# When the indirect writes of a routed block leave the GpSimd queue

## The chip, the cores and the metric

The kernel runs on one core of a Trainium2 chip. The metric is the device time of one execution in microseconds (us). A core has five engines with a queue each: TensorE (PE in the profile, its weight loads PEld), VectorE (DVE), ScalarE (ACT), GpSimd (POOL) and SyncE (SP, here only for DMAs). Each runs its queue in order, and they meet at semaphores.

## The reference, cut to what matters

16 sequences of 512 rows with 128 features are normalised and go through two branches, whose sum is added to the input: attention with 16 heads of 64, and a layer of 8 experts of which each row uses two.

```python
xn = layernorm(x)                                     # (16, 512, 128)
h = rmsnorm(xn) * norm_scale
q, k, v = h @ wq, h @ wk, h @ wv                      # 16 heads of 64
attn = softmax(q * 64**-0.5 @ k.T) @ v @ w_out + b_out
logits = silu(xn @ rw1 + rb1) @ rw2 + rb2             # the router, 8 experts
k_prob = softmax(top2(logits))
ffn = sum over the two chosen e of k_prob * (silu(xn @ w1[e] + b1[e]) @ w2[e] + b2[e])
out = x + attn + ffn
```

## The kernel before, in words

**Groups.** The program is written as 262 groups, `group(G)`. Of these, 256 carry attention: a batch has 16 groups (`GB`), a pair of heads has two (even and odd), and each group does two of the four tiles of 128 query rows. For each tile t: `scores` (PE, L394) fills two banks of PSUM; `maxima` (DVE, L403) reduces both to negated maxima NM; `probs` (ACT, L409) makes two tiles of exponentials; and in the group after, `turn_probs` (PE, L424) turns these with 16 transposes of 64x64, which ACT or DVE copies into PT (L436, L439). `weighted` (L453) multiplies PT by V. `project` (kq, L238 to L240) makes the next pair's queries or keys. Below, S0 and S1 are the scores of a group's two tiles, T0 and T1 the transposes of the group before, turned in between, and the first and second maximum those over S0 and S1.

**Order on TensorE.** `PE_ORDER` is written by hand: even groups run S0 T0 S1 T1 kq spread attend ... route, odd ones S0 T0 S1 ahead spread T1 route kq attend ... weighted. DVE and ACT have such lists too (`DVE_ORDER`, `ACT_ORDER`); POOL and SP take their work in the order in which it is added. PSUM banks are given out by a planner (`take`, with the costs in `HOLD`) as the work is added.

**The routed half.** In the groups 0 to 127, block r of 512 rows is routed over 8 groups, h = G mod 8, in `route(G)`. Groups h = 0 and 2: two chunks each of the router's first layer (`router`: PE L238 to L240 with XT, ACT tanh and bias, then on POOL `TH` L561 and `HS` L563). h = 3: `stats` of block r + 1 (DVE, then a POW on POOL, L284). h = 5 and 6: logits. h = 7: the first choice, and `turn_x(r + 1)` (PE, L338), which needs the first product of `routed_rows`. One block later, at h = 0 and 1, the second choice and `place` (DVE) make for each row its place in the list of its expert, and a flag (`gate` 24, L660) says that the places are there.

**The writes.** `scatter(r - 1, part)` then writes the rows of block r - 1 into the experts' lists in DRAM (`slots`): eight indirect DMAs from POOL (L664), one for each of the two choices and each of four tiles of 128 rows, 132 floats a row. They go out three in group h = 2, three in h = 3 and two in h = 4, all behind the flag alone. `routed_rows(r + 1)` (POOL, L307 to L313: three passes over 512 elements and two iotas) follows in h = 4. Its first instruction waits until all eight writes have landed, since it overwrites the rows that they read. In odd groups `route` is added ahead of `attend`, so every second block `attention_rows` (POOL, L298 and L300) stands behind `routed_rows`.

**Other work on POOL.** In the groups 24 to 57 (blocks 3 to 6 and the start of 7) `splitting` prepares the experts' weights; in even groups its subtraction (`SPL` L264) stands ahead of the writes. After the last routed block, in group 130, the eight writes of block 15 go out at once. From group 138 on the experts run beside attention, with accumulating indirect writes from POOL (L813, L534).

```python
elif 2 <= h <= 4:
    scatter(r - 1, slice(3 * h - 6, 3 * h - 3))   # 3, 3, 2 writes
...
if h == 4:
    routed_rows(r + 1)
```

Of the kernel before, what the change touches and what calls it, by code (L numbers as in the profile page):

```python
# [22 lines left out]
QT = S // P  # L23
# [42 lines left out]
class Queues:  # L66
# [7 lines left out]
    def add(self, engine, make, needs=(), name=None, step=1, sem=None, place="side"):  # L74
        key = None
        if name is not None:
            key = sem or (engine + "_" + name[0])
            self.count.setdefault(key, 0)
        self.open[engine].append((place, make, [n for n in needs if n is not None], name, key, step))
# [23 lines left out]
def block_kernel(nc, x, wq, wk, wv, wout, ns, bout, rw1, rb1, rw2, rb2, w1, w2, bias, ident, tri, consts, out):  # L103
# [11 lines left out]
    with ExitStack() as ctx:  # L115
# [111 lines left out]
        def load_q(r):  # L227
            if r < NB:
                add("sp", lambda e: e.dma_start(XQ[:, r % 2], xv[r]), needs=[("xc", r - 2), ("bn", r - 2)] if r >= 2 else [],
                    name=("xq", r), step=16, sem=f"xq_{r % 2}")  # L230
# [42 lines left out]
        def stats(r):  # L273
            for t in range(QT):
                add("dve", lambda e, t=t: e.bn_stats(bn[:, t, :], XQ[:, r % 2, t, :]),
                    needs=[("xq", r), ("mv", r - 1) if r else None], name=("bn", r))
            for t in range(QT):
                add("dve", lambda e, t=t: e.bn_aggr(mv[:, r, t, :], bn[:, t, :]), needs=[("bn", r)], name=("mv", r))
            old = ("pow", r - 1) if r else None
            add("dve", lambda e: e.tensor_scalar(sqi[:, 0:QT], mv[:, r, :, 1], 1.0, 1e-5, ALU.mult, ALU.add),  # L280
                needs=[("mv", r), old], name=("var", r, 0))
            add("dve", lambda e: e.tensor_scalar(sqi[:, QT:2 * QT], mv[:, r, :, 1], 1.0 + 1e-6, 1e-11, ALU.mult, ALU.add),
                needs=[("mv", r), old], name=("var", r, 1))
            add("pool", lambda e: e.tensor_tensor(sqo[:, r], sqi[:], HALF[:], ALU.pow), needs=[("var", r, 1), ("half",)],  # L284
                name=("pow", r))
# [16 lines left out]
        def routed_rows(r):  # L302
            mean = mv[:, r, :, 0:1].to_broadcast(full)
            rx = sqo[:, r, 0:QT].unsqueeze(2).to_broadcast(full)
            a, c = (XR[:, r % 2, k, :, 0:D] for k in range(2))
            old = [("sc", r - 2), ("xT", r - 2)] if r >= 2 else []
            add("pool", lambda e: e.tensor_tensor(c, XQ[:, r % 2], mean, ALU.subtract), needs=[("mv", r), ("xq", r), *old],  # L307
                name=("xc", r))
            add("pool", lambda e: e.tensor_tensor(a, c, rx, ALU.mult), needs=[("xc", r), ("pow", r), *old], name=("xr", r, 0))
            add("pool", lambda e: e.tensor_tensor(c, c, rx, ALU.mult), needs=[("xr", r, 0)], name=("xr", r, 1))  # L310
            for k in range(2):
                tok = XR[:, r % 2, k, :, D:D + 1].bitcast(I32)
                add("pool", lambda e, tok=tok: e.iota(tok, [[P, QT], [0, 1]], base=r * S, channel_multiplier=1),  # L313
                    needs=[*old, ("spare",)], name=("tok", r))
# [234 lines left out]
        def router(r, c):  # L549
            bk = xbank("r1")  # L550
            w = [R1[:, k, c * P:(c + 1) * P] for k in range(2)]
            m = [XT[:, k, :] for k in range(2)]
            add("pe", lambda e: three(e, bank[bk], w, m), needs=[("xTs", r, 1), ("wlo", "r1", 0), freed.get(bk)],
                name=("r1", r, c))
            add("act", lambda e: e.activation(TH[:, c % 2, :], bank[bk], ACT.Tanh, bias=RB1H[:, c:c + 1], scale=0.5),
                needs=[("r1", r, c), ("rb1h",), ("hs", r, c - 2) if c >= 2 else (("hs", r - 1, c + 2) if r else None)],
                name=("th", r, c))
            add("act", lambda e: e.activation(HS[:, c, :], bank[bk], ACT.Identity, bias=RB1[:, c:c + 1]),  # L558
                needs=[("r1", r, c), ("load", "rb1"), ("lg", r - 1) if r else None], name=("hz", r, c))
            freed[bk] = ("hz", r, c)  # L560
            add("pool", lambda e: e.tensor_tensor(TH[:, c % 2, :], TH[:, c % 2, :], HS[:, c, :], ALU.mult),  # L561
                needs=[("th", r, c), ("hz", r, c)], name=("tz", r, c))
            add("pool", lambda e: e.tensor_tensor(HS[:, c, :], HS[:, c, :], TH[:, c % 2, :], ALU.add),  # L563
                needs=[("tz", r, c)], name=("hs", r, c))

        def logits(r):
            bk = xbank("lg")

            def make(e):
                for c in range(NC):  # L570
                    m = e.matmul(bank[bk][32 * c:32 * c + 32, :], R2[:, c, :], HS[:, c, :], start=True, stop=True,
                                 tile_position=(0, 32 * c))
                return m

            add("pe", make, needs=[("hs", r, NC - 1), ("load", "r2"), freed.get(bk)], name=("lg", r))
            add("dve", lambda e: e.tensor_scalar(LG4[:], bank[bk], 0.5, RB2[:], ALU.mult, ALU.add),
                needs=[("lg", r), ("load", "rb2"), ("lgT", r - 1) if r else None], name=("lgs", r))
            freed[bk] = ("lgs", r)
# [3 lines left out]
        def turn_logits(r):  # L582
            bk = xbank("lgT")

            def make(e):
                for t in range(QT):
                    m = e.transpose(bank[bk][:, t * P:(t + 1) * P], LG4[:, t * P:(t + 1) * P], idn[:])
                return m

            add("pe", make, needs=[("lgs", r), ("load", "id"), freed.get(bk)], name=("lgT", r))  # L590
            parts = bank[bk].rearrange("p (t c e) -> p t e c", t=QT, c=NC)[:, :, 0:E]
            add("dve", lambda e: e.tensor_reduce(LG[:], parts, AX.X, ALU.add),
                needs=[("lgT", r), ("gate", r - 1, 6) if r else None], name=("gate", r, 0))
            freed[bk] = ("gate", r, 0)
# [64 lines left out]
                    needs=[("tanh", r), ("spare",), ("sc", r - 2) if r >= 2 else None], name=("wt", r, k))  # L659
            add("dve", lambda e: e.tensor_copy(junk[:, 2:3], junk[:, 0:1]), needs=[("to", r, 1), ("wt", r, 1)], name=("gate", r, 24))  # L660

        def scatter(r, part):
            for k, t in list(itertools.product(range(2), range(QT)))[part]:
                add("pool", lambda e, k=k, t=t: e.indirect_dma_start(  # L664
                    slots, bass.IndirectOffsetOnAxis(ap=IDX[:, r % 2, k, t:t + 1], axis=0), XR[:, r % 2, k, t, :], None),
                    needs=[("gate", r, 24), ("tok", r), ("xr", r, 1)], name=("sc", r), step=16, sem=f"sc_{r % 2}")

# [181 lines left out]
        for k in range(WARM):  # L851
            add("pe", lambda e: e.matmul(bank[7][:, 0:256], PR[:, 7, 0:P], PR[:, 7, 0:256], start=True, stop=True),
                needs=[("ones",)], name=("warm",))
# [8 lines left out]
        for key in (True, False):  # L862
# [12 lines left out]
            needs=[("pad0",)], name=("pad",))  # L875
# [56 lines left out]
        def route(G):  # L932
            r, h = divmod(G, 8)
            if 0 < r <= NB:
                if h == 0:
                    choose(r - 1, 1)
                    choose(r - 1, 2)
                if h == 1:
                    place(r - 1)
                if r == NB:  # L940
                    if h == 2:
                        scatter(r - 1, slice(0, 8))
                elif 2 <= h <= 4:
                    scatter(r - 1, slice(3 * h - 6, 3 * h - 3))
            if r >= NB:
                return
            if h in (0, 2):
                router(r, h)
                router(r, h + 1)
            if h == 5:  # L950
                logits(r)
                load_q(r + 2)
            if h == 6:
                turn_logits(r)
            if h == 7:
                choose(r, 0)
            if r + 1 < NB:
                if h == 3:
                    stats(r + 1)
                if h == 4:  # L960
                    routed_rows(r + 1)
                if h == 7:
                    turn_x(r + 1)
# [178 lines left out]
```

How the kernel before makes its waits and increments, by code:

```python
    def emit(self, engine, eng, sems):  # L91
        seen = {}
        for make, needs, key, step in self.items[engine]:
            for sem, value in (self.value[n] for n in needs):
                if seen.get(sem, 0) < value:
                    eng.wait_ge(sems[sem], value)
                    seen[sem] = value
            ins = make(eng)
            if key is not None:
                ins.then_inc(sems[key], step)
# [974 lines left out]
        @block.sync  # L1075
        def _(eng):
            q.emit("sp", eng, sems)
            for k, v in q.count.items():
                if k.startswith(("st_", "sadd", "spare_out", "base", "rrow", "tab", "b_tab", "sc_", "pads")):
                    eng.wait_ge(sems[k], v)
```

## Time and profile before

| | |
|---|---|
| three runs | 2043.05 to 2044.08 us, median 2043.65 us |
| profiled execution | 2040.24 us |
| its span, first to last instruction | 2038.4 us |
| mean granted TensorE clock | 0.990 |
| PE busy | 1947.9 us (96%) |
| DVE busy | 1539.4 us (76%) |
| ACT busy | 1574.2 us (77%) |
| POOL busy | 918.2 us (45%) |
| indirect writes to `slots` (L664) | 128, 125.8 us in all, 983 ns each |

Busy time is the union of an engine's instructions. The ends of matmuls are modelled in the profile, so when a result really was there is read from the engine that waits for it. The span of an indirect write on POOL is the time in which POOL prepares the transfer, not that of the transfer itself.

### The profile page before, as it was taken

How to read it: one execution, taken by the hardware profiler on the slowest of the kernel's cores; microseconds unless marked ns; L12 is line 12 of the kernel's file. 1: busy time of each engine (PE TensorE's matmuls, PEld its weight loads, DVE VectorE, ACT ScalarE, POOL GpSimd, SP SyncE). 2: the span in 40 equal slices, each digit the busy share in tenths (PEclk: the TensorE clock that was granted, in tenths of full speed). 3: DMA queues.
4: the chain of work that ended last, by engine and by line, in shares of the span. 5: the costliest groups of instructions: out<-in, count | busy, mean ns of one | idle time of the engine just before them, and what ended most of it. 6: DMA issues, size and time to landing. Idle time of an engine off the chain costs nothing.

```text
span 2038.4 us, 45230 instructions
## 1 busy us (share of the span) xinstructions
PE 1947.9 (96%) x16646; PEld 1254.4 (62%) x16646; DVE 1539.4 (76%) x2654; ACT 1574.2 (77%) x3716; POOL 918.2 (45%) x790
## 2 busy tenths in 40 slices
PE   7999999999999999998889999999999999999997
PEld 5655555555656555564556666666666666666664
DVE  6878888887878777776767777777777777777774
ACT  5777777777777777775678888888888888888884
POOL 4344455453344444441014645546446455464454
PEclk9999999999999999999999999999999999999999
DMA  2023222221111111001313334344333343343332
GB/s 84 30 61 103 91 98 89 85 72 34 40 37 43 38 43 38 33 32 36 91 57 81 84 86 84 80 95 85 85 79 85 86 83 88 84 85 80 79 75 47
DMA packets 132697, 141.96 MB, mean 70 GB/s; under 512 B 25438, under 2 KB 99038, under 8 KB 132446
## 3 DMA queue, kind: packets, MB, share of 16 engines
q1 hardware_dynamic: 101886, 118.34, 18.4%
q0 software_dynamic: 30592, 20.73, 8.6%
q8 instruction: 134, 2.20, 0.5%
q14 instruction: 85, 0.70, 0.1%
HBM read 102.65 MB, written 38.46 MB: 69 GB/s over the span
## 4 chain that ended last, share of the span: by engine, by line
PE 75%; ACT 12%; DVE 6%; issue 4%; DMA 2%; another core or an unknown queue 1%; SPq 0%; POOL 0%; POOLq 0%; DVEq 0%; ACTq 0%
PE pair L453 21%; PE pair L394 15%; PE pair L424 10%; PE pair L238 6%; PE pair L240 5%; PE pair L239 4%; ACT PR L409 4%; PE pair L499 2%; PE pair L501 2%; DVE NM L403 2%; PE pair L787 1%; PE pair L788 1%; PE pair L786 1%; ACT PT L436 1%; ACT HS L558 1%
## 5 line engine op out<-in xcount | busy, mean ns | idle before, releaser
L409 ACT ACTIVATE PR<-pair,NM 128x512 f32<-128x512 f32 x1024 | 718.2, 722 | 21.3 <-DVE NM L403 18.8
L403 DVE TENSOR_REDUCE NM<-pair 128x2 f32<-128x1024 f32 x512 | 611.8, 1211 | 68.0 <-PE pair L394 47.9
L436 ACT COPY PT<-pair 128x512 f32<-128x512 f32 x640 | 358.2, 608 | 368.4 <-PE pair L424 364.4
L394 PE MATMUL pair<-KS,QS 64*128 64x512 f32 x3072 | 491.7, 424 | 20.5 <-DVE KS L379 12.3
L453 PE MATMUL pair<-PT,V 128*64 128x512 f32 x2048 | 471.0, 602 | 0.2
L424 PEld LDWEIGHTS pair<-idn,PR 64*128 64x128 f32 x8192 | 338.0, 139 | 100.8 <-ACT HS L558 27.0
L394 PEld LDWEIGHTS pair<-KS,QS 64*128 64x128 f32 x3072 | 257.8, 188 | 181.1 <-issue 126.2
L424 PE MATMUL pair<-idn,PR 64*128 64x64 f32 x8192 | 343.2, 223 | 21.0 <-ACT HS L558 15.9
L813 POOL DMA_INDIRECT out<-YS,IDW x156 | 246.9, 1583 | 187.2 <-DVE YS L805 128.6
L778 POOL TENSOR_TENSOR HH<-ZZ,HH 128x512 fp32r<-128x512 f32 x156 | 199.2, 1347 | 291.1 <-ACT HH L775 291.1
L453 PEld LDWEIGHTS pair<-PT,V 128*64 128x64 f32 x2048 | 136.4, 137 | 258.7 <-issue 252.5
L439 DVE COPY PT<-pair 128x512 f32<-128x512 f32 x384 | 250.8, 681 | 14.7 <-remote 9.6
L409 ACT ACTIVATION_READ_ACCUMULATOR PR<-pair,NM 128x1 f32 x1024 | 242.1, 236 | 0.0
L561 POOL TENSOR_TENSOR TH<-TH,HS 128x512 f32<-128x512 f32 x64 | 81.8, 1278 | 295.9 <-ACT HS L558 295.6
L459 DVE TENSOR_TENSOR OT<-pair,RB 128x512 f32<-128x512 f32 x128 | 88.4, 690 | 144.8 <-PE pair L453 136.2
L772 DVE SCALAR_TENSOR_TENSOR ZZ<-ZT,ZZ 128x512 f32<-128x512 f32 x156 | 110.5, 709 | 79.2 <-ACT ZZ L763 79.1
L664 POOL DMA_INDIRECT slots<-XR,IDX x128 | 125.8, 983 | 89.9 <-DVE junk L660 58.8
L379 DVE TENSOR_TENSOR QS<-pair,QS 128x512 fp32r<-128x512 f32 x128 | 88.5, 691 | 90.0 <-ACT QS L378 87.7
L761 ACT ACTIVATE ZT<-pair,BT 128x512 f32<-128x512 f32 x156 | 116.6, 747 | 1.5 <-PE pair L240 1.4
L763 ACT ACTIVATE ZZ<-pair,BT 128x512 f32<-128x512 f32 x156 | 117.7, 754 | 0.0
L379 DVE TENSOR_TENSOR KS<-pair,KS 128x512 fp32r<-128x512 f32 x128 | 87.3, 682 | 9.3 <-ACT KS L378 9.1
L378 ACT CAST QS<-pair 128x512 fp32r<-128x512 f32 x128 | 77.9, 609 | 15.6 <-PE pair L240 9.3
(168 smaller groups left out, 2807.9 us busy)
## 6 DMA issues: line engine op xcount, KB each, us to landing
E<-w_tab SPq DMA_DIRECT2D x78, 512.0 KB
RB<-l_rows SPq DMA_DIRECT2D x127, 256.0 KB
XG<-slots SPq DMA_DIRECT2D x39, 264.0 KB
w_tab<-SPL SPq DMA_DIRECT2D x16, 512.0 KB
l_rows<-RT SPq DMA_DIRECT2D x508, 1.0 KB
xin<-in_x SPq DMA_DIRECT2D x16, 256.0 KB
XQ<-in_x SPq DMA_DIRECT2D x16, 256.0 KB
RAW<-in_w SPq DMA_DIRECT2D x16, 256.0 KB
```

Source lines behind the costliest of these rows:

```text
L238: e.matmul(ps, w[1], m[0], start=True, stop=False)
L379: add("dve", lambda e: e.tensor_tensor(lo, bank[bk], hi, ALU.subtract), needs=[(name + "hi", n), *old], name=(name + "lo", n), place="low")
L394: m = e.matmul(bank[bk + j], a[half[j], cols], c[half[j], :], start=(k == 0), stop=(k == 2))
L403: add("dve", lambda e: e.tensor_reduce(NM[:, 2 * t:2 * t + 2], both[:], AX.X, ALU.max, negate=True), needs=[("S", n, t), *([("exp", n - 1, ...
L409: add("act", lambda e: e.activation(PR[:, k, :], bank[bk], ACT.Exp, bias=NM[:, k:k + 1], accum_out=RS[:, n % 2, j, t:t + 1]), needs=[("max ...
L424: m = e.transpose(bank[two[r]][:, at:at + DH], PR[rows, 2 * t + j, c * P:(c + 1) * P], idn[rows, rows])
L436: add("act", lambda e, r=r: e.copy(dst[r], src[r]), needs=[("T", n, t), *old], name=("PT", n, t, r), place=f"turn{t % 2}")
L439: add("dve", lambda e, r=r: e.tensor_copy(dst[r], src[r]), needs=[("T", n, t), *old], name=("PT", n, t, r), place=f"turn{t % 2}")
L453: m = e.matmul(bank[bk][j * DH:(j + 1) * DH, :], V[:, k, h * DH:(h + 1) * DH], PT[:, n % 2 * 2 + j, k, :], start=(k == 0), stop=(k == QT - 1))
L664: add("pool", lambda e, k=k, t=t: e.indirect_dma_start(slots, bass.IndirectOffsetOnAxis(ap=IDX[:, r % 2, k, t:t + 1], axis=0), XR[:, r % 2 ...
L778: add("pool", lambda e: e.tensor_tensor(lo, ZZ[:, r], hi, ALU.subtract), needs=[("hi", n), old], name=("lo", n))
L813: add("pool", lambda e, t=t: e.indirect_dma_start(out, bass.IndirectOffsetOnAxis(ap=IDW[:, i % 4, t, 0:1].bitcast(U32), axis=0), YS[:, i % ...
```

## The change

The eight writes go out in four groups, h = 2 to 5, two in each. Each pair carries one more wait a write: the first waits for the group's first maximum, the second for its second. `routed_rows(r + 1)` moves from h = 4 to h = 5. The writes of the last block (group 130) stay as they were.

```diff
-        def scatter(r, part):
-            for k, t in list(itertools.product(range(2), range(QT)))[part]:
+        def scatter(r, part, behind):
+            for (k, t), start in zip(list(itertools.product(range(2), range(QT)))[part], behind):
                 add("pool", lambda e, k=k, t=t: e.indirect_dma_start(
                     slots, bass.IndirectOffsetOnAxis(ap=IDX[:, r % 2, k, t:t + 1], axis=0), XR[:, r % 2, k, t, :], None),
-                    needs=[("gate", r, 24), ("tok", r), ("xr", r, 1)], name=("sc", r), step=16, sem=f"sc_{r % 2}")
+                    needs=[("gate", r, 24), ("tok", r), ("xr", r, 1), start], name=("sc", r), step=16, sem=f"sc_{r % 2}")
...
                     if h == 2:
-                        scatter(r - 1, slice(0, 8))
-                elif 2 <= h <= 4:
-                    scatter(r - 1, slice(3 * h - 6, 3 * h - 3))
+                        scatter(r - 1, slice(0, 8), [None] * 8)
+                elif 2 <= h <= 5:
+                    scatter(r - 1, slice(2 * h - 4, 2 * h - 2), [("max", G // 2, 2 * (G % 2) + t) for t in range(2)])
...
-                if h == 4:
+                if h == 5:
                     routed_rows(r + 1)
```

## Rows read from the trace of the kernel before

**Rows 1.** Stretches of blocks 10 and 15: us, busy (count) per engine, PEclk, DMA, GB/s.

```profile
597.00:655.00 58.00, 55.58 (x514) 34.53 (x510) 46.67 (x96) 43.03 (x107) 25.06 (x24) 1.00 0.12 38
...
885.00:947.00 62.00, 57.24 (x502) 35.01 (x498) 44.28 (x84) 42.44 (x105) 17.92 (x16) 0.94 0.10 31
```

**Rows 2.** PE's waits, 60 to 940 us: who waited for whom, total, times, longest.

```profile
PE pair L238 <- ACT PT L436: 12.1, 9, 1.4
PE pair L394 <- DVE PT L439: 5.4, 5, 3.3
PE pair L238 <- issue: 3.8, 10, 0.6
```

**Rows 3.** Timeline, block 10, group h = 4: start, us, engine, instruction [idle before <- releaser].

```profile
623.26 1.01 POOL L664 DMA_INDIRECT slots<-XR,IDX  x1 [0.15 <-issue]
...
624.58 0.95 POOL L664 DMA_INDIRECT slots<-XR,IDX  x1 [0.30 <-issue]
...
624.94 0.66 PE L424 MATMUL pair<-idn,PR 64*128 64x64 f32 x16
...
625.23 1.18 DVE L403 TENSOR_REDUCE NM<-pair 128x2 f32<-128x1024 f32 x1
...
625.83 0.96 POOL L664 DMA_INDIRECT slots<-XR,IDX  x1 [0.30 <-issue]
626.18 0.65 PE L424 MATMUL pair<-idn,PR 64*128 64x64 f32 x16
626.82 1.67 POOL L284 TENSOR_TENSOR sqo<-sqi,HALF 128x8 f32<-128x8 f32 x1
627.53 1.07 ACT L436 COPY PT<-pair 128x512 f32<-128x512 f32 x2 [4.04 <-PE pair L424]
...
628.17 0.50 PE L238 MATMUL pair<-HT,WK 128*128 128x512 f32 x1 [1.34 <-ACT PT L436]
...
630.02 0.96 POOL L664 DMA_INDIRECT slots<-XR,IDX  x1 [0.30 <-issue]
...
632.06 1.07 ACT L436 COPY PT<-pair 128x512 f32<-128x512 f32 x2 [0.27 <-PE pair L424]
```

**Rows 4.** Timeline of block 10, group h = 2, with the first writes.

```profile
610.13 1.03 POOL L664 DMA_INDIRECT slots<-XR,IDX  x1 [1.67 <-DVE junk L660]
...
611.05 1.18 DVE L403 TENSOR_REDUCE NM<-pair 128x2 f32<-128x1024 f32 x1
...
611.99 0.66 PE L424 MATMUL pair<-idn,PR 64*128 64x64 f32 x16
...
613.74 1.23 DVE L403 TENSOR_REDUCE NM<-pair 128x2 f32<-128x1024 f32 x1 [1.51 <-remote]
```

**Rows 5.** Timeline of DVE, maxima of block 10, groups h = 3 and 5.

```profile
617.91 2.46 DVE L403 TENSOR_REDUCE NM<-pair 128x2 f32<-128x1024 f32 x2 [0.55 <-PE pair L394]
...
632.27 2.35 DVE L403 TENSOR_REDUCE NM<-pair 128x2 f32<-128x1024 f32 x2
```

**Rows 6.** Timeline in the experts' half: one indirect write (L813) beside transposes.

```profile
1140.06 0.66 PE L424 MATMUL pair<-idn,PR 64*128 64x64 f32 x16
1140.15 1.76 POOL L813 DMA_INDIRECT out<-YS,IDW  x1 [3.93 <-DMA out<-xin,TOK]
...
1141.51 1.07 ACT L436 COPY PT<-pair 128x512 f32<-128x512 f32 x2 [0.39 <-PE pair L424]
```

**Rows 7.** Timeline of block 10: the next rows on POOL, and their transposes.

```profile
635.29 1.04 POOL L307 TENSOR_TENSOR XR<-XQ,mv 128x512 f32<-128x512 f32 x1 [4.31 <-DMA slots<-XR,IDX]
...
647.53 0.66 PE L338 MATMUL pair<-idn,XR 128*128 128x128 f32 x4
```

**Rows 8.** Timeline of DVE, block 15, where five writes go out together.

```profile
918.55 1.22 DVE L403 TENSOR_REDUCE NM<-pair 128x2 f32<-128x1024 f32 x1 [4.22 <-remote]
```

**Rows 9.** Timeline of PE, same stretch of block 15.

```profile
921.02 1.65 PE L394 MATMUL pair<-KS,QS 64*128 64x512 f32 x6 [3.27 <-DVE PT L439]
```

**Rows 10.** Timeline of POOL, block 5: the splitting ahead of the first writes.

```profile
328.54 1.29 POOL L264 TENSOR_TENSOR SPL<-RAW,SPL 128x512 fp32r<-128x512 f32 x1 [9.91 <-ACT SPL L263]
```

## The prediction

> **What bounds the kernel now.** I read four views in this order. The page's busy times first: PE is busy for 96% of the span, no other engine for more than 77%, and a stretch of the routed half says the same (55.58 of 58 us on PE against 46.67 on DVE) [rows 1]. So time is lost where PE stands still, and PE's waits are the second view. In the routed half three of them bear on this change: 12.1 us in 9 waits before a projection, until ACT has copied transposed tiles out of their banks; 5.4 us before scores, until DVE has done such copies; 3.8 us before projections with no releaser named [rows 2]. Together 21.3 us.
>
> Third, the timeline shows what is late there. In group h = 4 of block 10, T0 leaves PE at 624.94 + 0.66 = 625.60, but the copy that only needs T0 begins at 627.53, 1.93 later, after 4.04 us in which ACT had nothing to do [rows 3]. The projection behind it wants the bank and starts at 628.17, after 1.34 us of idle PE; 9 times 1.34 is the 12.1 us of rows 2. One group later the same copy waits 0.27 us [rows 3]. What differs is POOL: three indirect writes begin at 623.26, 624.58 and 625.83, so two of them lie on T0 and T1, while the last write of the block, from 630.02, lies on projections and delays nothing [rows 3]. In group h = 2 three writes from 610.13 on do the same: the first maximum ends at 612.23, the second begins only at 613.74 [rows 4]. In block 15, where five go out together, the maximum waits 4.22 us and PE 3.27 us [rows 8, 9]. So a result of PE is handed on late when transposes run among back-to-back indirect writes. Fourth, the single write: in the experts' half one that starts 0.09 us after a group of transposes makes their copy begin at 1141.51 instead of 1140.72, 0.79 us late [rows 6]. So one write is cheap and a train of three is not.
>
> **The change part by part.** Times are those of block 10; whatever is gained moves all later ones forward alike.
>
> *h = 2, first pair.* The first write no longer starts at 610.13 but behind the first maximum, at 612.23 plus the 0.30 us that POOL leaves between writes [rows 3, 4], about 612.5. T0 is then through. T1 leaves PE at 611.99 + 0.66 = 612.65 [rows 4], so 0.1 us of it still meets the write. The second maximum follows the first at once, ends near 612.23 + 1.23 = 613.46, and the second write starts near 613.8, beside projections, until the next group's scores, whose first maximum begins at 617.91 [rows 5]. Price: between nothing (the quiet copy of rows 3) and 0.79 (rows 6); I take 0.1, as almost all of T1 is over. Behind these waits POOL's queue holds the router's four products of the same group. They are not ready before ACT has done its tanh, which comes after PE's last part of the group; in block 10 they were being worked on right up to 623.1, as the 0.15 us of idle time ahead of the write at 623.26 shows [rows 3]. The waits end nearly ten us earlier, so nobody waits for them.
>
> *h = 3, second pair.* Its maxima ended at 617.91 + 2.46 = 620.37 [rows 5], before POOL gets there. So here the new waits hold nothing back, and the writes start at 623.26 and 624.58 as now. What goes is the third write at 625.83. T0 still lies beside the second one (624.58 to 625.53). Bounds for its lateness without the third: 0 and 0.79; I take 0.3, since this write ends before T0 does and that of rows 6 runs on for 1.19 us. The projection starts 0.64 us after the copy (627.53 to 628.17), and PE is busy with T1 until 626.83, so the copy may begin 0.59 us after T0 before PE stands still. At 0.3 the idle 1.34 us are gone; at 0.79 0.2 us would stay.
>
> *h = 4, third pair.* The POW (1.67 us) now follows the fourth write at once, 625.56 to 627.23 [rows 3]. The first maximum of the group ended at 625.23 + 1.18 = 626.41, the second, no longer late, ends near 627.64. The writes run from about 627.5 and 628.8: behind T1, and done by 629.8, as far ahead of the next group's T0 as the last write is now. Price nothing.
>
> *h = 5, last pair, and the next rows.* The maxima of h = 5 end at 633.5 and 632.27 + 2.35 = 634.62 [rows 5], so the last write starts near 634.9. The landing, now 630.02 to 635.29 or 5.27 us [rows 3, 7], ends near 640.2. Then come the two products that `turn_x` needs, 1.1 us each, done by 642.4. PE asks for them at 647.53 [rows 7], so 5.1 us of cover remain. Behind the waiting `routed_rows` POOL's queue holds `attention_rows` in every second block, wanted only in group 9 of 16. SP's queue is passed by nothing: the step that moves issues no DMA, and the rows that `load_q` replaces have been read a block earlier.
>
> *Blocks 3 to 6.* There the first writes also stand behind the weight splitting, which waits 9.91 us for ACT [rows 10], so POOL comes a group late, finds the maxima done and still writes beside transposes, in pairs instead of threes. Of the 5.4 us, 3.3 are block 15's; of the other 2.1 I keep half, 1.1.
>
> *Block 15.* Five writes become two and two apart. Its 3.27 us of idle PE are in the 21.3. Besides, its granted clock was 0.94 over 62 us [rows 1], that is 3.7 us, and the scores right behind the idle stretch took 1.65 us [rows 9]. Without the idle stretch I expect no fall.
>
> *Sum.* 21.3 - 1.1 + 3.7 = 23.9 us off the profiled 2040.24 us, or 2016.3. The median of the runs stands 3.4 us above that execution, so I forecast 2020 us. The upper bound takes 0.2 us of idle PE at three places in 14 blocks (8.4), the kept half of 2.1 again (1.1) and no clock gained (3.7): 2033. Below, the second maximum of h = 2 is 1.51 us late in some nine blocks, of which rows 2 show only a part as idle PE; if 0.9 more each came back, 2012.
>
> **A rule that speaks against it.** The trace has T0's copy 1.93 us late beside the writes and 0.27 us behind PE without them [rows 3]. The Trainium skill, "SBUF — State Buffer", section "SBUF: two separate sides", says that engine accesses and DMA accesses use separate ports and cannot slow each other, and that the only contended pair is that of GpSimd and VectorE; TensorE never waits for anyone. By that rule the writes cannot be what makes transposes late, and moving them gives nothing; by the rows it gives 23.9 us. That outcome is the second rival.
>
> **The rivals.**
> 1. *Two writes are enough.* Write 4 covers T0 of h = 4 almost whole. If two in a row delay it as three do, the 12.1 us stay: 2020 + 12 = 2032. For it: the second maximum of h = 2 was late with just two writes ahead of it and the third running [rows 4]. Against: the single write's 0.79.
> 2. *The writes are not the cause.* The lateness belongs to those groups for a reason that stays, such as the bank planner's choices, and PE's idle time remains: 2044. For it: the releaser of the late maximum is named "remote", so the row itself doesn't name a write [rows 4]. Against: block 15, with five writes, has the longest wait [rows 8].
> 3. *The next rows come too late.* With `routed_rows` a group later, PE waits at `turn_x`. It decides once landing takes more than 5.27 + 5.1 = 10.4 us, and outweighs the gain past 12.1 us (14 blocks times 1.7). At 13 us: 14 times 2.6 is 36, less 24: 2056, slower. Against it: 5.27 is what a landing takes now, in a group in which SP also loads denominators.
> 4. *The clock.* Every idle stretch lands elsewhere in time; six more falls like that of block 15, 3.7 us each, would eat 22: 2042.
>
> **How the numbers follow.** Chances: forecast 0.67, two writes enough 0.15, not the cause 0.08, next rows late 0.06, the clock 0.04. The time is the forecast's, 2020. Its own range, 2012 to 2033, holds the first rival too; the others stay out with 0.18, so I give 2011 to 2035. A measurement of this kernel tells 0.2%, or 4 us, from no change: faster 0.83 (the first two and a part of the fourth), same 0.10, slower 0.07.
>
> **What would show it.** Right: PE's waits for ACT's copies before projections fall from 12.1 us to below 3; in h = 4 the copy begins within 0.6 us of T0's end; in h = 2 the second maximum follows the first without a gap; block 15 keeps its clock. Wrong: copies still 1 us or more late with two writes ahead (first rival); late maxima though POOL is idle (second); a wait of PE before L338 (third). The prediction fails if the idle time of rows 2 goes and the span shortens by less than 15 us.

## The result, and the profile after

The changed kernel takes 2019.14 us (median of 4 runs, 2017.40 to 2020.34) against 2043.45 us of the kernel before (4 runs, 2043.05 to 2044.08): ratio 0.9883 [0.9872, 0.9895]. Forecast were 2020. Its profiled execution took 2020.23 us, span 2018.4, 20.0 less than the profiled one before.

PE's waits of the routed half, 60 to 940 us (who waited for whom, total, times, longest), answer [rows 2]:

```profile
PE pair L424 <- ACT HS L558: 15.2, 16, 1.3
PE pair L394 <- DVE PT L439: 2.4, 5, 1.4
PE pair L238 <- issue: 0.5, 2, 0.3
```

The 12.1 us before projections are gone altogether, the 5.4 became 2.4, the 3.8 became 0.5. The first row is the wait for the router's ACT work, which was there before and is there in every run below.

The timeline of block 10 answers [rows 3 to 5, 7] (start, us, engine, instruction, idle time before and its releaser):

```profile
604.03 2.38 DVE L403 TENSOR_REDUCE NM<-pair 128x2 f32<-128x1024 f32 x2
...
604.98 0.66 PE L424 MATMUL pair<-idn,PR 64*128 64x64 f32 x16
...
606.03 1.03 POOL L664 DMA_INDIRECT slots<-XR,IDX  x1 [4.58 <-DVE NM L403]
...
615.79 1.01 POOL L664 DMA_INDIRECT slots<-XR,IDX  x1 [0.16 <-issue]
617.10 0.95 POOL L664 DMA_INDIRECT slots<-XR,IDX  x1 [0.30 <-issue]
...
617.47 0.65 PE L424 MATMUL pair<-idn,PR 64*128 64x64 f32 x16
...
618.67 1.07 ACT L436 COPY PT<-pair 128x512 f32<-128x512 f32 x2 [2.65 <-PE pair L424]
...
619.30 0.50 PE L238 MATMUL pair<-HT,WK 128*128 128x512 f32 x1
...
619.94 1.03 POOL L664 DMA_INDIRECT slots<-XR,IDX  x1 [0.19 <-issue]
...
624.89 0.95 POOL L664 DMA_INDIRECT slots<-XR,IDX  x1 [2.66 <-DVE NM L403]
...
629.36 1.04 POOL L307 TENSOR_TENSOR XR<-XQ,mv 128x512 f32<-128x512 f32 x1 [2.24 <-DMA slots<-XR,IDX]
...
638.65 0.66 PE L338 MATMUL pair<-idn,XR 128*128 128x128 f32 x4
```

In h = 2 both maxima run back to back from 604.03 on, where DVE stood idle for 1.51 us before the second; T1 ends at 604.98 + 0.66 = 605.64, before the first write begins at 606.03. In h = 4, T0 ends at 617.47 + 0.65 = 618.12 and its copy begins at 618.67, 0.55 late instead of 1.93; the projection at 619.30 shows no idle time ahead of it. The last pair waits for its maximum (2.66 us).

The clock, by stretches (us, busy and count per engine, PEclk, DMA, GB/s), answers [rows 1]; the third is the stretch of the last block's eight writes, which the change left alone:

```profile
593.80:649.30 55.50, 54.62 (x498) 33.85 (x497) 46.07 (x95) 42.41 (x105) 25.07 (x24) 1.00 0.12 40
870.20:927.10 56.90, 54.27 (x493) 33.33 (x493) 44.09 (x84) 42.26 (x105) 17.94 (x16) 1.00 0.10 34
930.00:960.00 30.00, 21.42 (x161) 12.65 (x158) 18.30 (x45) 14.00 (x36) 9.74 (x10) 0.83 0.10 33
```

Block 15 keeps its clock (1.00 instead of 0.94). Below, the time of a block is measured from its first exponential (L409) to that of the next block, an even measure of what a block costs. For blocks 8 to 14 it was 57.4 to 58.0 us before and is 55.5 to 55.8 after; block 15 went from 61.96 to 56.95.

### The profile page after: what moved, and what is told of

Its sections match the earlier page's. It is cut to its first block, busy times and chain, and to the rows that moved or that the text cites. A ratio compares the mean times of both kernels' runs of the same rounds, so it can differ in the third digit from the quotient of the medians.

```text
span 2018.4 us, 45230 instructions
## 1 busy us (share of the span) xinstructions
PE 1951.1 (97%) x16646; PEld 1257.6 (62%) x16646; DVE 1540.0 (76%) x2654; ACT 1573.7 (78%) x3716; POOL 918.1 (45%) x790
## 4 chain that ended last, share of the span: by engine, by line
PE 78%; ACT 11%; DVE 4%; issue 3%; DMA 2%; another core or an unknown queue 1%; SPq 0%; POOL 0%; POOLq 0%; ACTq 0%; DVEq 0%
PE pair L453 22%; PE pair L394 16%; PE pair L424 11%; PE pair L238 7%; PE pair L240 5%; PE pair L239 5%; ACT PR L409 4%; PE pair L499 3%; PE pair L501 3%; PE pair L787 1%; PE pair L788 1%; PE pair L786 1%; DVE NM L403 1%; ACT HS L558 1%; ACT V L359 1%
## 5 line engine op out<-in xcount | busy, mean ns | idle before, releaser
L409 ACT ACTIVATE PR<-pair,NM 128x512 f32<-128x512 f32 x1024 | 718.1, 722 | 19.1 <-DVE NM L403 17.1
L394 PE MATMUL pair<-KS,QS 64*128 64x512 f32 x3072 | 490.3, 423 | 15.1 <-DVE KS L379 10.2
L813 POOL DMA_INDIRECT out<-YS,IDW x156 | 246.7, 1581 | 186.7 <-DVE YS L805 127.8
L409 ACT ACTIVATION_READ_ACCUMULATOR PR<-pair,NM 128x1 f32 x1024 | 241.8, 236 | 0.0
L378 ACT CAST KS<-pair 128x512 fp32r<-128x512 f32 x128 | 76.8, 600 | 18.6 <-PE pair L240 10.6
```

The source lines that it names most:

```text
L394: m = e.matmul(bank[bk + j], a[half[j], cols], c[half[j], :], start=(k == 0), stop=(k == 2))
L409: add("act", lambda e: e.activation(PR[:, k, :], bank[bk], ACT.Exp, bias=NM[:, k:k + 1], accum_out=RS[:, n % 2, j, t:t + 1]), needs=[("max ...
L813: add("pool", lambda e, t=t: e.indirect_dma_start(out, bass.IndirectOffsetOnAxis(ap=IDW[:, i % 4, t, 0:1].bitcast(U32), axis=0), YS[:, i % ...
```

## Experiments

Kernels of one occasion ran one after the other on one chip, together with the kernel before. Two theories were held against each other. **A**: trains of indirect writes on POOL make PE's results be handed on late, and the change gains by drawing them apart. **B**: something else is late in those groups, or the gain is of the order of the work, and the writes only happen to stand there.

### The change taken apart, and a surprise

Four kernels on chip 14, five rounds each: the pairs without their waits; the old threes with waits; the old threes with only the next rows later; the pairs behind scores in place of maxima.

```diff
# pairs_no_max
+ scatter(r - 1, slice(2 * h - 4, 2 * h - 2), [None] * 2)
# threes_behind_max
+ elif 2 <= h <= 4:
+     scatter(r - 1, slice(3 * h - 6, 3 * h - 3), [("max", G // 2, 2 * (G % 2) + t) for t in (0, 1, 1)])
# rows_late_only: the kernel before, but for
+ if h == 5:
+     routed_rows(r + 1)
# pairs_behind_scores
+ scatter(r - 1, slice(2 * h - 4, 2 * h - 2), [("S", G // 2, 2 * (G % 2) + t) for t in range(2)])
```

> The change without its waits: pairs in h = 2 to 5, next rows in h = 5, no write behind a maximum. Theory (a train of indirect writes that POOL prepares beside transposes hands PE's results late, and from the third in a row on PE stands idle): h = 2 and 3 keep most of the gain, since a pair is short, but nothing holds the pair of h = 5 back, so in most blocks four writes go out in a row from h = 4 on and run into the transposes of h = 5: 0.3 to 1.3 us of idle PE a block over 14 blocks, 2024 to 2037 us. Rival A (the waits behind the maxima are the whole gain): back to 2041 to 2044. Rival B (the later next rows are the gain): 2018 to 2021.

> The waits without the pairs: 3, 3 and 2 writes in h = 2 to 4, the first of each group behind the first maximum and the others behind the second, next rows in h = 4 as before. Theory: h = 2 becomes quiet (2 to 3 us in all) and block 15 loses a part of its train of five (2 to 7 us), but the three writes of h = 3 find their maxima done and go out in a row beside T0 and T1 of h = 4, so the 1.34 us a block stay: 2033 to 2040 us. Rival A (the waits are the whole gain): 2018 to 2022. Rival B (the later next rows): 2041 to 2044.

> The kernel before with the next rows asked for in h = 5 instead of h = 4 and nothing else. Theory: POOL's order of work is the same and the rows wait for the landing anyway, 2042 to 2045 us. Rival B: most of the gain, 2018 to 2025. If the later rows cost something, over 2046.

> The changed kernel with each write behind the scores of its tile instead of behind the maximum over them, so about 1.2 us earlier. Theory: in h = 2 and h = 5 the pair now meets T0 and T1; two such pairs a block at 0.2 to 0.6 us of idle PE each, 2023 to 2034 us. Rival C (only the number in a row matters, not what runs on PE meanwhile): 2018 to 2021, like the changed kernel.

Measured: 1998.91, 1999.02, 1997.49 and 1999.03 us, ratios 0.9999 [0.9990, 1.0008], 0.9998 [0.9989, 1.0006], 0.9994 [0.9984, 1.0005] and 0.9999 [0.9990, 1.0010]. These are the times of neither theory: the kernel before itself took 1999.68 us there (35 runs, 1995.80 to 2005.87), 44 us less than at first. Nothing was late. The timeline of the kernel that keeps the threes, the same writes on the same transposes as in [rows 3]:

```profile
608.15 1.01 POOL L664 DMA_INDIRECT slots<-XR,IDX  x1 [0.15 <-issue]
609.46 0.96 POOL L664 DMA_INDIRECT slots<-XR,IDX  x1 [0.30 <-issue]
609.84 0.65 PE L424 MATMUL pair<-idn,PR 64*128 64x64 f32 x16
...
610.54 1.07 ACT L436 COPY PT<-pair 128x512 f32<-128x512 f32 x2 [2.15 <-PE pair L424]
610.73 0.95 POOL L664 DMA_INDIRECT slots<-XR,IDX  x1 [0.30 <-issue]
```

T0 ends at 610.49 and its copy begins 0.05 us later, not 1.93, with a write running before, beside and after it. Blocks 8 to 14 take 55.2 to 55.5 us in all four kernels. So the writes are not enough by themselves: there is a condition under which results are handed on late, and it was absent here. Which part of the change matters could not be read from these runs.

### The change itself, once more

The unchanged new kernel, on chip 8 and on chip 6, three rounds each.

> The changed kernel itself, unaltered, beside the kernel before on whichever chip this call gets. Theory (the change removes late deliveries of PE's results and nothing else): where the kernel before runs near 2043 us, 2017 to 2021 us again; where it runs near 1999 us there are no late deliveries to remove, so no difference beyond 4 us. Rival D (the gain has another cause, and that chip hides it in some other way, such as a faster experts' half): 20 us or more faster than the kernel before on every chip, so 1975 to 1980 us where that one runs near 1999.

> The changed kernel once more, to tell a chip's own trait from an accident of one occasion. Where PE's results are handed on late (the kernel before at 2037 to 2044 us): 2018 to 2022 us, ratio 0.987 to 0.993. Where they are not (the kernel before at 1999 to 2001 us): 1999 to 2001 us, ratio 0.999 to 1.001. A rival by which the gain belongs to one chip or one moment and not to lateness expects a ratio within 0.998 to 1.002 beside a kernel before of 2037 us or more.

Measured: 2000.03 us against 2000.21, ratio 1.000 [0.999, 1.001], and 1998.91 against 1999.25, ratio 0.9998 [0.9988, 1.0007]. Where nothing is late the change gives nothing, and costs nothing. Later next rows are no loss either.

### More writes, on purpose

The changed kernel, with four more indirect writes (into a scratch table) in each block's group h = 0.

```diff
+ if h == 0 and 1 <= r <= 14:
+     extra(r, ("qlo", G // 2))      # four indirect writes from POOL
```

> The changed kernel with four more indirect writes a block in 14 blocks, of a constant tile to a scratch tensor, in group h = 0 behind the low halves of the queries of the group before, so that they run through S0, T0, S1 and T1 of h = 0. A dose by itself. Theory, where the kernel before runs near 2043 us: 1.3 to 3 us of idle PE in each of 14 blocks, 18 to 42 us above the changed kernel, 2037 to 2061 us. Where it runs near 1999 us, PE's results are not handed late by any number of writes: 1996 to 2004 us. Rival (a chip without late deliveries merely has a higher limit, which four in a row and four more a block exceed): copies of T0 and T1 in h = 0 late by 1 us or more, 2010 us or more there too.

Measured on chip 8: 2015.19 us, ratio 1.0077 [1.0057, 1.0097]. That misses the 1996 to 2004 us expected and lies where the rival had it, but the rival's cause is not there: no copy was late, and blocks 8 to 14 took 55.2 to 55.5 us, as without the writes. The time went in blocks 4 to 7, 59.75, 60.93, 59.34 and 62.26 us against 55.79, 56.37, 55.79 and 55.89 in the changed kernel of chip 6. There the extra writes stand behind the weight splitting, and push the router's products on POOL (L562 and L564 in this kernel) onto DVE's chain of `place`. Its timeline:

```profile
439.74 1.28 POOL L562 TENSOR_TENSOR TH<-TH,HS 128x512 f32<-128x512 f32 x1
439.79 1.27 DVE L653 TENSOR_TENSOR gt<-gt 128x32 f32<-128x32 f32 x1
...
441.09 1.27 POOL L564 TENSOR_TENSOR HS<-HS,TH 128x512 f32<-128x512 f32 x1
...
441.32 1.07 DVE L657 CAST IDX<-gm 128x4 uint32<-128x4 f32 x1
...
444.95 1.11 PE L425 MATMUL pair<-idn,PR 64*128 64x64 f32 x16 [3.44 <-DVE OT L460]
```

Two of DVE's small operations end with POOL's product beside them: 439.79 + 1.27 = 441.06 against 439.74 + 1.28 = 441.02, and 442.39 against 442.36. The same two take 0.18 to 0.60 and 0.17 us in the changed kernel without the extra writes. DVE comes late to the attention output and PE stands still for 3.44 us. That is another cost of moving POOL's work, and not that of [rows 3].

### All arrangements in one kernel

To have every arrangement under one condition, whichever that was, one kernel gave each block its own.

```diff
+ HOW = [..., "threes", "pairs_max", "pairs", "threes_max", "pairs_scores", "threes", "pairs_max", ...]   # blocks 8 to 14
+ EXTRA = {1: "sp", 2: "pool", 14: "indirect"}   # four more transfers in h = 0
```

> One kernel with the arrangement of the writes changed from block to block, to have all doses in one trace: blocks 3, 5, 7, 8 and 13 threes as before; 1, 2, 4, 6, 9, 14, 15 pairs behind maxima as changed; 10 pairs without a wait; 11 threes behind maxima; 12 pairs behind scores; the last eight in threes behind maxima. Four more writes beside the transposes of h = 0 in block 1 (plain, from SP), 2 (plain, from POOL) and 14 (indirect, from POOL). Where the kernel before runs near 2043 us, theory: the block takes (from the first exponential of its h = 0) 57.4 to 57.7 us with threes (8, 13), 55.5 to 55.8 as changed (9), 56 to 57.5 with pairs alone (10) and pairs behind scores (12), 56.8 to 57.4 with threes behind maxima (11), 57 to 59 with the indirect extra (14), 55.5 to 56 with the extra from SP (1), and with the plain extra from POOL (2) as much as with the indirect one if the preparation on POOL counts, as little as from SP if it is the indirect kind. Where the kernel before runs near 2000 us: 55.2 to 55.5 us in all of the blocks 8 to 14, and no copy of transposed tiles late.

> The mixed kernel once more, on whatever chip it meets, to have all arrangements under one condition. Theory (trains of writes make PE's results late, where a chip shows lateness at all): if the kernel before needs some 2043 us beside it, the blocks with threes (8, 13) take 57.4 to 58.0 us and their copy in h = 4 begins 1.9 us after T0, the changed one (9) takes 55.5; pairs without a wait (10) tell the first rival: 57.4 if two writes do what three do, 55.5 to 56 if not; threes behind maxima (11) take 55.5 to 56.5 if placing alone would do; block 14, with four more indirect writes, is late in h = 0 too, by 1 to 2 us; four plain transfers from POOL (block 2) or SP (block 1) cost nothing if it is POOL's preparation of an indirect write that counts. If the kernel before needs some 1999.5 us, nothing is late and every block from 8 to 14 takes 55.2 to 55.5 us, as in the first look. Rival (the lateness belongs to certain groups, not to the writes): 57.4 in the blocks whatever the arrangement, where the kernel before needs 2043 us.

First on chip 8: 1996.84 us beside 1999.38 of the kernel before (one run each), all blocks 8 to 14 at 55.27 to 55.48. Then on chip 9 the condition was there: 2022.21 beside 2037.69. A third kernel, with the arrangements in other blocks, met it as well, on chip 8 of all: 2022.40 beside 2039.23. (These are single runs; what counts is the comparison of blocks inside one execution.)

```diff
+ HOW = [..., "threes_max", "pairs", "pairs_max", "threes", "pairs_max", "pairs_scores", "threes", ...]   # blocks 8 to 14
+ EXTRA = {12: "indirect"}
+ # the last eight writes three, three and two behind maxima; the adds of the experts' half behind maxima
```

> The mixed kernel with the arrangements in other blocks (8: threes behind maxima, 9: pairs without a wait, 10: the change, 11: threes, 12: the change with four more indirect writes in h = 0, 13: pairs behind scores, 14: threes), the last eight writes spread as in the earlier experiment, and the adds of the experts' half behind maxima. If the kernel before needs 2037 us or more beside it: theory, the extra time of a block goes with its arrangement, over 55.3 us in even and 55.45 in odd blocks: threes 2.1 to 2.4 us, threes behind maxima about 1.7, pairs behind scores 1.2, pairs 1.0, the change 0.2, the four extra writes 2.0 more; and in the experts' half copies behind the adds are late no longer. Rival: it goes with the block (9 stays at 55.7, 8 at 57.7). If the kernel before needs about 1999.5 us: 55.3 to 55.5 us in every block from 8 to 14, total 1996 to 2001 us.

Time of a block in us, its number in front:

| writes of the block | chip 9 | chip 8, other order | chip 8, nothing late |
|---|---|---|---|
| threes (as before) | 8: 57.70; 13: 57.54* | 14: 57.38; 11: 57.56* | 8: 55.28; 13: 55.46 |
| threes behind maxima | 11: 57.12 | 8: 56.91 | 11: 55.44 |
| pairs behind scores | 12: 56.43 | 13: 56.19 | 12: 55.27 |
| pairs, no wait | 10: 56.32 | 9: 59.81 | 10: 55.29 |
| pairs behind maxima (the change) | 9: 55.68 | 10: 55.50 | 9: 55.48 |
| the change, and four more in h = 0 | 14: 56.15, and 1.30 in 13 | 12: 56.21, and 1.31 in 11 | 14: 55.27 |

(* The extra writes of the following block begin in this one's last group, which took 8.79 and 8.81 us instead of 7.49 and 7.50; the difference is taken off here and put into the last row.)

The time goes with the arrangement and not with the block: block 8 cost 57.70 with threes and 56.91 with threes behind maxima, 9 cost 55.68 with the change and 59.81 with bare pairs. B falls. Over 55.28 us for even and 55.46 for odd blocks, threes cost 2.1 to 2.4 us, the change 0.2. Bare pairs leave 1.0 in block 10 and threes with waits 1.6 to 1.7, so both parts are needed: of the 2.2 us, going out in twos brings some 1.2 and waiting for the maxima the last 0.8 or more. These two shares rest on block 10 alone: the 56.32 us lie between the 55.5 to 56 and the 57.4 expected there, and the other block of bare pairs took 59.81. Waiting for the scores instead of the maxima leaves 1.15 and 0.73 (1.2 was expected for the second), little or no better than no wait. Four more writes in a group that had none cost 2.0 us each time, 1.3 in the group in which they begin and 0.7 in the next. Of the plain transfers, those from SP in block 1 were issued between transposes. Those from POOL in block 2 had left POOL at 132.90, just before T0, but were still on their way beside it; the last landed at 134.21:

```profile
130.63 2.27 POOL L681 DMA_DIRECT2D scratch<-PAD  x4 [6.99 <-DVE QS L383]
...
133.03 0.66 PE L428 MATMUL pair<-idn,PR 64*128 64x64 f32 x16
...
133.72 1.07 ACT L440 COPY PT<-pair 128x512 f32<-128x512 f32 x2 [2.07 <-PE pair L428]
```

T0 ends at 133.69 and its copy begins 0.03 us later, so the transfers alone made nothing late there. What POOL's preparing of a plain transfer does beside transposes was not met.

The timeline of the kernel on chip 9 shows how, in blocks 8 (threes), 9 (the change) and 10 (bare pairs):

```profile
506.64 1.01 POOL L668 DMA_INDIRECT slots<-XR,IDX  x1 [0.16 <-issue]
...
507.95 0.96 POOL L668 DMA_INDIRECT slots<-XR,IDX  x1 [0.30 <-issue]
508.32 0.66 PE L428 MATMUL pair<-idn,PR 64*128 64x64 f32 x16
...
509.22 0.96 POOL L668 DMA_INDIRECT slots<-XR,IDX  x1 [0.30 <-issue]
...
510.94 1.07 ACT L440 COPY PT<-pair 128x512 f32<-128x512 f32 x2 [4.06 <-PE pair L428]
...
511.58 0.50 PE L242 MATMUL pair<-HT,WK 128*128 128x512 f32 x1 [1.37 <-ACT PT L440]
...
565.52 0.96 POOL L668 DMA_INDIRECT slots<-XR,IDX  x1 [0.30 <-issue]
565.89 0.66 PE L428 MATMUL pair<-idn,PR 64*128 64x64 f32 x16
...
567.05 1.08 ACT L440 COPY PT<-pair 128x512 f32<-128x512 f32 x2 [2.61 <-PE pair L428]
...
623.78 1.04 POOL L668 DMA_INDIRECT slots<-XR,IDX  x1 [0.19 <-issue]
...
627.66 0.96 POOL L668 DMA_INDIRECT slots<-XR,IDX  x1 [0.30 <-issue]
628.03 1.07 ACT L440 COPY PT<-pair 128x512 f32<-128x512 f32 x2 [1.30 <-PE pair L428]
629.49 1.23 DVE L407 TENSOR_REDUCE NM<-pair 128x2 f32<-128x1024 f32 x1 [1.06 <-remote]
```

The first part is the three of block 8: T0 ends at 508.98, but its copy begins at 510.94, 1.96 late and 0.76 after the end of the last write (510.18). The next is block 9, the change: the same T0, but the train ends with the write at 565.52; the copy begins at 567.05, 0.57 after that write's end (566.48) and 0.50 after T0's. So in these two T0's result comes 0.6 to 0.8 us after the train is through. That is no rule: in h = 2 of [rows 4], T0's copy began at 612.21, while the train ran on to 613.70. The last part is block 10, bare pairs: the third and the fourth pair (623.78 to 628.62) run into each other and make one train of four over T0 of the next group, whose second maximum waits 1.06 us. The maxima keep those two pairs apart.

In block 9 of the third kernel this train of four fell so that T0's copy came 2.7 us late, at 572.06, and the clock fell behind it. Its timeline and its stretches:

```profile
568.61 0.71 PE L428 MATMUL pair<-idn,PR 64*128 64x64 f32 x16
...
570.01 0.96 POOL L668 DMA_INDIRECT slots<-XR,IDX  x1 [0.30 <-issue]
572.06 1.07 ACT L440 COPY PT<-pair 128x512 f32<-128x512 f32 x2 [2.50 <-PE pair L428]
...
572.79 1.26 PE L575 MATMUL pair<-HS,R 128*32 128x512 f32 x8 [1.95 <-ACT PT L440]
```

```profile
565.00:568.50 3.50, 3.50 (x33) 2.54 (x29) 3.28 (x6) 3.50 (x10) 2.96 (x3) 1.00 0.10 29
568.50:572.00 3.50, 2.34 (x42) 1.97 (x38) 1.69 (x2) 1.06 (x3) 1.91 (x2) 1.00 0.89 222
572.00:575.40 3.40, 2.61 (x11) 1.02 (x11) 1.82 (x2) 2.42 (x6) 0.00 (x0) 0.72 0.16 52
575.40:579.00 3.60, 3.60 (x15) 1.23 (x16) 1.35 (x2) 2.42 (x6) 3.09 (x4) 0.79 0.04 11
```

PE was busy for 2.34 of 3.50 us, then its granted clock was 0.72 and 0.79. The wait of 1.95 us and the low clock behind it are the greater part of what block 9 lost (59.81 over 55.46). It is why this number is not used for the price of bare pairs above; but they did cost it, so the price found for them is 1.0 us in one block and 4.4 in the other.

### What is left: the last eight, and the adds

In the changed kernel the last block's eight writes still go out at once. Its timeline:

```profile
936.38 0.95 POOL L664 DMA_INDIRECT slots<-XR,IDX  x1 [29.44 <-DVE junk L660]
...
942.40 1.22 DVE L403 TENSOR_REDUCE NM<-pair 128x2 f32<-128x1024 f32 x1 [3.91 <-remote]
...
945.21 0.96 POOL L664 DMA_INDIRECT slots<-XR,IDX  x1 [0.30 <-issue]
948.14 1.29 DVE L439 COPY PT<-pair 128x512 f32<-128x512 f32 x2 [4.52 <-remote]
...
950.17 1.65 PE L394 MATMUL pair<-KS,QS 64*128 64x512 f32 x6 [8.27 <-DVE KS L379]
```

The second scores ended at 938.43 and their maximum begins at 942.40; T1 ended at 938.92 and its copy begins at 948.14, 9.2 us late. PE stands still for 8.27 us and then works at the low clock (1.65 us for a scores group, as in [rows 9]). Two kernels draw these writes apart, the second one also the accumulating writes of the experts' half.

```diff
# last_eight_spread, groups 130 to 132
+ if 2 <= h <= 4:
+     scatter(r - 1, slice(3 * h - 6, 3 * h - 3), [("max", G // 2, 2 * (G % 2) + t) for t in (0, 1, 1)])
# last_eight_and_adds, besides
+ add_rows(i, (2 * c, 2 * c + 1), ("max", G // 2, 2 * (G % 2) + c) if G < GROUPS else None)
```

> The changed kernel with the eight writes of the last block spread as well: three, three and two in groups 130 to 132, behind the maxima of the group, instead of eight in a row in group 130. In the run of the kernel before on this occasion's chip the time tells first whether results of PE are handed on late there at all: near 2043 us they are, near 2000 us they are not, as on the chip of the four runs before. Where they are late, theory: the train of eight (8.27 us of idle PE and 10.2 us at the lower clock behind it) goes, 5 to 12 us below the changed kernel, 2008 to 2014 us. Where they are not: no difference from the kernel before beyond 4 us. Rival (PE's idle time in group 131 belongs to the totals that VectorE works out there): no gain on either chip.

> The changed kernel, with two more trains put behind maxima: the last block's eight writes go out three, three and two, each behind a maximum of its group, and the two accumulating writes of a tile of rows in the experts' half wait for a maximum too. Where results are handed on late: last block from 58 to 56 us or so and up to 8 us less in the experts' half by PE's waits there, against the waits that the adds may bring: 2008 to 2018 us, 2 to 10 us under the changed kernel. Where nothing is late: 1997 to 2002 us, no difference. Rival (the adds' waits hold up POOL's queue, on which the next gather stands): 2 to 10 us slower than the changed kernel on either kind of chip.

Both met nothing late: 1997.75 us, ratio 0.9991 [0.9977, 1.0005] (chip 0, one round), and 1998.69, ratio 0.9996 [0.9986, 1.0006] (chip 6). But both mixed kernels carry the spread writes too, and where results were late their block 16 took 58.28 and 57.87 us, against 65.08 in the changed kernel and 63.67 in the one before. Block 17 gives a little of it back (70.53 and 70.68 against 69.92 in the changed kernel), so some 6 us are still to be had under the condition. The adds are not: PE's waits for ACT's copies before projections are 4.4 us from 960 us on in the kernel on chip 9 and 4.3 in the third one, with the adds behind maxima: the expectation that no copy would be late behind them failed. The change with the last eight spread was not run under the condition as a kernel of its own.

## Why the prediction was right

**The mechanism** was the one forecast: trains of indirect writes beside transposes make PE's results late, and the second rival (not the writes) fell when the lateness moved with the writes from block to block. The trace says it once more: it keeps the time of every semaphore signal, which the views above do not print. In the kernel before, the signal of T0 in [rows 3] comes at 627.51, 0.02 us ahead of its copy; so it is PE's signal that is late, not ACT that is slow. The second maximum of [rows 4], with its releaser "remote", waits for such a signal too, that of S1 (612.15), at 613.72. Of PE's 2064 signals that can be told apart in that trace, 113 come more than 0.3 us after the modelled end of their matmuls. All 113 matmuls ended during an indirect write on POOL or up to 0.8 us behind one; of the 1492 that ended farther off, none is among them. The transposes are hit most, 73 of 134 groups that ended so near a write, against 24 of 136 scores, 13 of 200 projections and none of 43 products with V. No signal of DVE, ACT or POOL in this trace is over 0.1 us late, and where nothing was late (the mixed kernel on chip 8) none of PE's 2108 is.

The Trainium skill, "SBUF — State Buffer", section "SBUF: two separate sides", by which a transfer cannot slow an engine and TensorE waits for nobody, is what the run on chip 14 shows (0.05 us late); where the condition is present, the row says 1.93. What the late time follows is POOL's preparing of the write rather than the transfer: in the kernel before, nothing moved on the DMA engines for most of the time in which the copy of [rows 6] was late: T0 ended at 1140.72, no packet moved until 1141.27, and the copy begins at 1141.51. No packet of POOL's queue moved in all of this time. Its stretches:

```profile
1140.40:1140.80 0.40, 0.40 (x13) 0.40 (x10) 0.40 (x2) 0.40 (x2) 0.40 (x1) 1.00 0.00 0
1140.80:1141.20 0.40, 0.40 (x6) 0.33 (x5) 0.40 (x1) 0.31 (x1) 0.40 (x1) 1.00 0.00 0
1141.20:1141.51 0.31, 0.31 (x12) 0.23 (x9) 0.31 (x1) 0.01 (x1) 0.31 (x1) 1.00 1.56 198
```

The plain transfers of block 2 above agree. That is argued from two places; no run was made to separate the two, and why preparing a write should hold back a signal of PE is not shown.

**The steps.** *h = 2*: 0.1 us forecast, none seen, since the first write begins 0.8 us behind the first maximum (604.03 + 1.18 = 605.21) and not 0.30. The margin of nearly ten us ahead of the router's products was misread: before the change the first of them began at 617.87, some 3 us behind the end forecast for the second write; after it POOL still stands idle for 2.06 us ahead of it. *h = 3*: 0.3 forecast, 0.55 seen, just inside the 0.59 of slack, so PE does not wait. The single write of 0.79 was a fair upper bound, and the first rival (two writes do what three do) is wrong for a pair by itself; for two pairs that meet it is right, as block 10 of the mixed kernel shows. *h = 4 and 5*: nothing, as forecast, in h = 5 only because of the waits; in h = 4 the pair comes behind the POW (0.19 us of idle time at 619.94), as forecast, and waits for no maximum. *The next rows*: the landing took 629.36 - 626.15 = 3.2 us instead of 5.27, and the cover before `turn_x` is 638.65 less 631.5, the end of the second product, or 7.1 us instead of 5.1. The third rival was far off. *Blocks 3 to 6*: 1.1 us of waits kept, forecast; up to 430 us four of the five waits for DVE's copies are left, 0.9 us in all. *Block 15*: its clock came as forecast, of its 3.27 us only 1.8, since the fifth of these waits, 1.4 us, is there. No next block is prepared in it, so no POW stands between the second pair and the third; that train of four was not foreseen.

**The sum** was too large by 3.9 us against the profiled execution: 23.9 forecast, 20.0 measured. PE's waits fell from 21.3 to 2.9, or by 18.4 where 20.2 were forecast. Blocks 1 to 15 took 844.1 us instead of 867.2, 23.1 less. But 1.4 were lost before block 1, where the start ran at a granted clock of 0.79 instead of 0.90 (14 to 38 us), and 1.7 from block 16 on: behind the last eight writes the low clock lasted 10.2 us (the 0.83 above) instead of 6.8. This is the term "clock", +3.7: right for block 15, and given back elsewhere, as the fourth rival had it in small. By chance the other bridge made good for it: the profiled execution stood 3.2 us below the median of the four runs before (2043.45) and 1.1 above it after, so the medians differ by 24.3.

**What the prediction could not see** is the condition. It took lateness for a property of the kernel. The kernel before takes 1998.6 to 2000.2 us on five occasions (chips 14, 0, 8, 8 and 6) and 2037.7 to 2043.5 on three, and the change was worth 24 us on the one of these three on which it ran by itself, and nothing on the two of the five on which it did. That the forecast was timed under the condition is luck: on five of eight occasions there was nothing to gain. What makes the difference stays open. It is not the chip's number, since chip 8 was seen in both. It held for all kernels of an occasion. It is not TensorE's clock, whose mean was 0.990 in the late run on chip 9 and 0.991 in the quiet one on chip 14. Nor do the instructions last longer: in the mixed kernel a write takes 963 ns in the median on chip 9 and 964 on chip 8, a copy of transposed tiles 592 on both.

## What to carry to other kernels

When an engine waits although its producer is done, ask which other engine is at work in just those gaps, and move that work to another place of the program: here the lateness went with the writes wherever they were put. Long trains are what costs where results are late at all, so tie each short one to an event that comes right after the sensitive stretch. And time the kernel before again on other occasions, before a gain of 1% is put down to the code alone.

## What was not expected of the hardware

- Results of PE were handed on late, by 1.93 and 1.96 us beside a train of three indirect writes and by 9.2 us beside eight, on three occasions of eight; on the other five not at all (0.05 us), with the same program.
- In the late trace of the kernel before only PE's signals were late, and only beside indirect writes or up to 0.8 us behind them; those of transposes most (73 of 134), those of products with V never (0 of 43).
- A late result of T0 in h = 4 came 0.6 to 0.8 us after the last write of the train, not after the write that it lies on. Elsewhere it came 1.1 us behind a train of four (572.06), 2 us behind one of eight (948.14), or while the train still ran (612.21).
- Two of DVE's small operations from SBUF to SBUF last until the product that POOL has under way ends: a product of two tensors (1.27 beside 1.28 us, against 0.18 to 0.60) and a cast (1.07 against 0.17). The reduction between them (L655) does not: its 32 executions all take 0.19 us. The Trainium skill, "SBUF — State Buffer", section "SBUF: two separate sides", says that these two engines share a port and that one locks the other out for a whole instruction; for these two operations this trace agrees.
